# Linear attention and expert layer on one core: the keys of blocks 1 to 15 transposed by VectorE and 16 transfers instead of by TensorE, and the first block's orders rewritten

## The reference, cut to what matters

```python
def chunked_linear_attn(q, k, v):           # per chunk of 64 rows, per head
    inter  = einsum('bhcd,bhde->bhce', qq, state)
    scores = einsum('bhcd,bhed->bhce', qq, kk) * mask
    intra  = einsum('bhce,bhed->bhcd', scores, vv)
    state  = state + einsum('bhcd,bhce->bhde', kk, vv)
...
x = x + layernorm(attn(layernorm(x)))       # attn: q, k, v, the chunks, a norm per head, Wo
x = x + layernorm(ffn(layernorm(x)))        # ffn: sum over 8 experts of weight * Wd(silu(Wg x) * Wu x)
```

## Time and profile before

| | |
|---|---|
| median of 3 runs | 1467.39 us (1464.14 to 1468.72) |
| the profiled execution | 1467.63 us |
| its span | 1465.9 us |
| mean granted TensorE clock | 0.995 |
| TensorE busy | 1443.0 us (98%) |
| VectorE busy | 1027.0 us (70%) |
| ScalarE busy | 613.9 us (42%) |
| GpSimd busy | 428.4 us (29%) |
| DMA, share of its 16 engines by the packets of the main queue | 9.1% |

### The profile page before, as it was taken

The page is one execution under the profiler, slowest core; times in us unless marked ns, Lnnn a source line. Parts: engine busy times, 40 slices in busy tenths (PEclk is TensorE's granted clock), DMA queues, the critical chain, the costliest instruction groups (busy, mean ns, idle before and its releaser), DMA issues. The chain is left out here.

```text
span 1465.9 us, 37265 instructions
## 1 busy us (share of the span) xinstructions
PE 1443.0 (98%) x14076; PEld 1254.8 (86%) x14076; DVE 1027.0 (70%) x2459; ACT 613.9 (42%) x1159; POOL 428.4 (29%) x607
## 2 busy tenths in 40 slices
PE   7899999999999999999999999999999999999997
PEld 6788888888888888888888888888888888888887
DVE  6657768586686767768676686867768676685765
ACT  5443534444343343534344344443434445344432
POOL 1322414134241232414134241232413134241230
PEclk9999999999999999999999999999999999999999
DMA  5210100101001010100101001010100101000000
GB/s 173 73 16 6 32 7 14 29 14 29 0 14 29 14 29 0 34 9 14 29 14 29 0 14 29 14 29 0 31 12 14 29 14 29 0 15 16 1 8 22
DMA packets 106945, 32.53 MB, mean 22 GB/s; under 512 B 83616, under 2 KB 106656, under 8 KB 106912
## 3 DMA queue, kind: packets, MB, share of 16 engines
q1 hardware_dynamic: 106912, 32.08, 9.1%
HBM read 23.60 MB, written 8.39 MB: 22 GB/s over the span
## 5 line engine op out<-in xcount | busy, mean ns | idle before, releaser
L878 ACT ACTIVATE late<-gate_ps 128x512 f32<-128x512 f32 x256 | 153.2, 599 | 282.4 <-PE gate_ps L495 282.3
L495 PE MATMUL down_ps<-w_hi,h_hi 128*128 128x256 f32 x976 | 264.9, 294 | 0.0
L775 ACT ACTIVATE h_hi<-late 128x512 fp32r<-128x512 f32 x256 | 161.6, 631 | 235.5 <-DVE late L1125 235.5
L495 PE MATMUL down_ps<-w_hi,h_lo 128*128 128x256 f32 x976 | 254.4, 283 | 0.0
L1125 DVE TENSOR_TENSOR late<-late,up_ps 128x512 f32<-128x512 f32 x256 | 174.9, 683 | 112.1 <-PE up_ps L495 109.6
L1372 POOL TENSOR_TENSOR rms_in<-rms_in,minus_half 128x16 f32<-128x16 f32 x32 | 93.7, 2928 | 491.5 <-DVE rms_in L1073 491.5
L987 DVE TENSOR_TENSOR h_lo<-late,h_hi 128x512 fp32r<-128x512 f32 x256 | 175.6, 686 | 59.7 <-ACT h_hi L775 59.7
L1147 DVE SCALAR_TENSOR_TENSOR late<-down_ps,route,late 128x256 f32<-128x256 f32 x364 | 158.4, 477 | 82.2 <-PE down_ps L495 79.7
L495 PE MATMUL gate_ps<-ft_hi,w_hi 128*128 128x512 f32 x512 | 202.8, 396 | 1.6 <-ACT late L878 1.5
L495 PE MATMUL gate_ps<-ft_hi,w_lo 128*128 128x512 f32 x512 | 202.8, 396 | 0.0
L495 PE MATMUL up_ps<-ft_hi,w_lo 128*128 128x512 f32 x512 | 199.4, 389 | 0.0
(11 more groups left out here) (185 smaller groups left out, 2381.9 us busy)
## 6 DMA issues: line engine op xcount, KB each, us to landing
xs<-in_x SPq DMA_DIRECT2D x32, 256.0 KB, 2.9
out_rows<-late SPq DMA_DIRECT2D x32, 256.0 KB, 2.2
kz<-in_x SPq DMA_DIRECT2D x240, 32.0 KB, 1.8
late<-in_wg SPq DMA_DIRECT2D x7, 256.0 KB, 3.4
late<-in_wu SPq DMA_DIRECT2D x7, 256.0 KB, 4.5
late<-in_wd SPq DMA_DIRECT2D x6, 256.0 KB, 3.4
var_o<-var_s SPq DMA_DIRECT2D x60, 1.0 KB, 1.8
late<-in_wkv_t SPq DMA_DIRECT2D x1, 512.0 KB, 4.2
```

The costliest lines, as they stand in the source:

```text
L495: last = nc.tensor.matmul(dst, lhs, rhs, start=n == 0, stop=n == len(terms + low_terms) - 1)
L775: return nc.scalar.activation(dst, src, ACT.Copy)
L878: nc.scalar.activation(h_f[:, m, :], gate_ps[:, :], ACT.Silu).then_inc(silu_ready[0], 1)
```

## The change

The step "kt" leaves the places of the loop. In its stead VectorE turns the 32x32 blocks of `k_sb` into `rows` (step "k_turn", 4 instructions, at place 5), and SyncE places the turned blocks with 16 transfers of 32 KB from `rows` into `k_t`, the first half of `kz`, whose layout is changed (`place_keys`). The scores wait for all 16 (`k_placed`) instead of for ScalarE's copies. "kv" 1 and "q" 0 change places, so that both halves of the keys are there earlier. On SyncE, `place_keys` stands at the head of a pass, ahead of `load_x_t`. The first block keeps TensorE's transposes; its tables of order are written anew, and the matmuls that take the mean of the attention weights become steps of the table.

```diff
 STEPS = [
-    [("kv", 0), ("q", 0)],
+    [("kv", 0), ("kv", 1)],
     [],
-    [("q", 1), ("kv", 1)],
-    [("keep_x1",)],
-    [("kt", 0), ("kt", 1)],
+    [("q", 0), ("q", 1)],
+    [("keep_x1",), ("k_turn",)],
+    [],
...
-FIRST_PE = [("xt", 0), ("xt", 1), ("kv", 0), ("kv", 1), ("q", 0), ("su", 0), ("kt", 0), ("su", 1), ("q", 1), ("kt", 1),
+FIRST_PE = [("mean", "wkv"), ("xt", 0), ("mean", "wq"), ("xt", 1), ("kv", 0), ("q", 0), ("kv", 1), ("su", 0), ("kt", 0),
...
-FIRST_ACT = [("high", "wkv"), ("high", "wq"), ("xt", 0), ("high", "wo"), ("unit", 0), ("unit", 1), ("unit", 2), ("xt", 1),
+FIRST_ACT = [("xt", 0), ("high", "wkv"), ("xt", 1), ("high", "wq"), ("high", "wo"), ("unit", 0), ("unit", 1), ("kv", 0),
...
-        kz = sb("kz", [P, 2, HG, 2, 2 * P])
-        x_blocks = kz[:, :, :, 1, :]
+        kz = sb("kz", [P, 2, 2, HG, 2 * P])
+        k_t = kz[:, 0, :, :, :].rearrange("p h g c -> p (h g c)").rearrange("p (n c) -> p n c", c=P)
+        k_blocks = rows[:, :, :].rearrange("p t n -> p (t n)").rearrange("p (n c) -> p n c", c=P)
+        x_blocks = kz[:, 1, :, :, :]
...
+            def place_keys(block):
+                reach(sp, k_turned, block, 0)
+                for n in range(P // 32):
+                    for j in range(HPG):
+                        sp.dma_start(k_t[D * j:D * j + D, :, 32 * n:32 * n + 32],
+                                     k_blocks[32 * n:32 * n + 32, :, D * j:D * j + D]).then_inc(k_placed[0], 16)
...
             with sp.Fori(1, BLOCKS - 1) as i:
+                place_keys((i, 0))
                 reach(sp, blocks_turned, (i, 0), 0)
                 load_x_t(i * ROWS + ROWS)
...
+            place_keys((BLOCKS - 1, 0))
             store_out((BLOCKS - 2, 0), (BLOCKS - 2) * ROWS)
...
-                elif kind == "kt":
-                    p = step[1]
-                    reach(pe, k_ready, a, p + 1)
-                    for b in range(B):
-                        for g in range(HG):
-                            last = nc.tensor.transpose(dst[:, g, b * P:b * P + P], k_sb[:, 2 * p + b, g * P:g * P + P],
-                                                       ident[:, :])
                 elif kind == "s":
                     p = step[1]
                     reach(pe, q_ready, a, p + 1 if is_first(a) else HG)
-                    reach(pe, kz_ready, a, p + 1)
-                    if not is_first(a):
+                    if is_first(a):
+                        reach(pe, kz_ready, a, p + 1)
+                    else:
+                        reach(pe, k_placed, a, 0)
...
+                elif kind == "k_turn":
+                    reach(dve, k_ready, a, 2)
+                    for t in range(TILES):
+                        last = nc.vector.transpose(rows[:, t, :], k_sb[:, t, :])
+                    last.then_inc(k_turned[0], 1)
```

More of the change, by code:

```diff
@@ L96 @@
[L96 to L102, removed]
@@ new lines @@
+FIRST_DVE = [("x_stats", 0), ("x_stats", 1), ("x_norm", 0), ("centre", "wkv"), ("x_norm", 1), ("xt", 0), ("low", "wkv"),
+             ("centre", "wq"), ("scale", "wo"), ("xt", 1), ("low", "wq"), ("low", "wo"), ("unit", 0), ("unit", 1),
+             ("unit", 2), ("unit", 3), ("unit", 4), ("unit", 5), ("unit", 6), ("su", 0), ("su", 1), ("unit", 7),
+             ("unit", 8), ("s", 0), ("unit", 9), ("unit", 10), ("s", 1), ("unit", 11), ("unit", 12), ("norm_stats", 0),
+             ("unit", 13), ("unit", 14), ("unit", 15), ("norm_stats", 1), ("unit", 16), ("norm_apply", 0), ("unit", 17),
+             ("unit", 18), ("ot", 0), ("norm_apply", 1), ("unit", 19), ("ot", 1), ("unit", 20), ("ln2_stats", 0),
+             ("ln2_stats", 1), ("ln2_add", 0), ("ln3_stats", 0), ("ln2_add", 1), ("ln3_stats", 1), ("ln3_norm", 0),
+             ("ln3_norm", 1), ("ft_out", 0), ("ft_out", 1), ("unit", 21)]
@@ L107 @@
+FIRST_POOL = [("x_stats", 0), ("x_stats", 1), ("norm_stats", 0), ("norm_stats", 1), ("ln2_stats", 0), ("carry", 0),
+              ("ln2_stats", 1), ("ln3_stats", 0), ("ln3_stats", 1)]
+FIRST_WARM = {("kv", 0): 4, ("ot", 0): 16, ("ot", 1): 8, ("ft", 0): 27, ("ft", 1): 3}
 ROUTER, ROUTER_T = ("r",), ("rt",)
@@ L111, in psum_steps @@
     return [s for after in steps for s in after
-            if s[0] in ("q", "kv", "kt", "s", "o", "su", "ot", "wo", "ft")] + [ROUTER, ROUTER_T]
-PSUM_STEPS, FIRST_PSUM_STEPS = psum_steps(STEPS), [s for s in FIRST_PE if s[0] != "xt"] + [ROUTER, ROUTER_T]
+            if s[0] in ("q", "kv", "s", "o", "su", "ot", "wo", "ft")] + [ROUTER, ROUTER_T]
+PSUM_STEPS, FIRST_PSUM_STEPS = psum_steps(STEPS), [s for s in FIRST_PE if s[0] not in ("mean", "xt", "kt")] + [ROUTER, ROUTER_T]
 N_PSUM = len(PSUM_STEPS)
@@ L233, in build_program @@
         blocks_turned = counter("blocks_turned", 1)
+        kt_done = sem("kt_done")
+        k_turned = counter("k_turned", 1)
+        k_placed = counter("k_placed", 16 * HPG * P // 32)
         xt_loaded = counter("xt_loaded", 16 * B * KT * P // 32)
@@ L543, in att_step @@
                     last.then_inc(xt_done, 1)
+                elif step[0] == "mean":
+                    n, raw, columns = (0, wkv_raw, 2 * HID) if step[1] == "wkv" else (1, wq_raw, HID)
+                    pe.wait_ge(att_w_loaded[1 - n], 16)
+                    for k in range(KT):
+                        last = nc.tensor.matmul(up_ps[n][:, 0:columns], rz, raw[:, k, :], start=k == 0, stop=k == KT - 1)
+                    last.then_inc(mean_done, 1)
+                elif step[0] == "kt" and is_first(a):
+                    p = step[1]
+                    reach(pe, k_ready, a, p + 1)
+                    for b in range(B):
+                        for g in range(HG):
+                            last = nc.tensor.transpose(halves(up_ps[p][:, :])[:, g, b * P:b * P + P],
+                                                       k_sb[:, 2 * p + b, g * P:g * P + P], ident[:, :])
+                    last.then_inc(kt_done, 1)
                 if step not in PSUM_STEPS:
@@ L550, in att_step @@
                     pass
+                elif is_first(a) and number < 2:
+                    pe.wait_ge(xt_ready[0], number + 1)
                 elif number >= 2:
@@ L594, in att_step @@
                         tok, out_c = 2 * p * P + c, (b * HG + g) * C
-                        last = nc.tensor.matmul(score_banks(p)[C * i:C * i + C, j, out_c:out_c + C], kz[head, p, g, 0, c:c + C],
+                        last = nc.tensor.matmul(score_banks(p)[C * i:C * i + C, j, out_c:out_c + C], k_t[head, 2 * (2 * p + b) + g, C * i:C * i + C],
                                                 q_t[head, g, tok:tok + C], start=True, stop=True)
@@ L604, in att_step @@
                                     last = nc.tensor.matmul(dst[C * i:C * i + C, r, (4 * b + n) * C:(4 * b + n) * C + C],
-                                                            kz[half, p, g, j, c:c + C], q_t[half, g, tok:tok + C],
+                                                            kz[half, j, p, g, c:c + C], q_t[half, g, tok:tok + C],
                                                             start=True, stop=True)
@@ L728, in _ @@
             pe.wait_ge(const_ready, 1)
[L729 to L734, removed]
+            warm(2)
             for step in FIRST_PE:
@@ L820, in att_step @@
                 elif kind == "kt":
-                    if not is_first(a):
-                        copy(kz[:, step[1], :, 0, :], src).then_inc(kz_ready[0], 1)
-                        return
+                    act.wait_ge(kt_done, step[1] + 1)
                     for j in range(2):
-                        last = nc.scalar.activation(kz[:, step[1], :, j, :], src, ACT.Copy, scale=odd_even[:, j:j + 1])
+                        last = nc.scalar.activation(kz[:, j, step[1], :, :], halves(up_ps[step[1]][:, :]), ACT.Copy,
+                                                    scale=odd_even[:, j:j + 1])
                     last.then_inc(kz_ready[0], 1)
```

17 lines of the change are left out of this document (7 added, 10 removed).

## The result

The change takes 1505.89 us (median of 4 runs, 1504.94 to 1506.58) against 1467.36 us for the kernel before (median of 4, 1464.14 to 1468.72): 1.0265 times as long, with an interval from 1.0248 to 1.0283, or 38.5 us more. The profiled execution took 1505.44 us, with a span of 1503.7 us and a mean granted clock of 0.985.

What follows compares the result with a forecast made beforehand. TensorE's list of work was taken to bound the kernel; 1467.6 - 13.2 (transposes) + 34.5 (waits for keys) + 16 (clock) - 3 (first block) = 1502 us, range 1474 to 1518.

Steps and rivals of the forecast that it cites:

- TensorE's list: In blocks 1 to 15, the 8 transposes leave TensorE: 0.88 us per block, 13.2 us less in all.
- The turn on VectorE: Four block transposes per block take 1.41 us and fit in VectorE's 1.34 us wait before the next `hidden`, costing nothing.
- The price of an issue: On SyncE, each of the 16 key transfers takes 0.66 us to issue, one behind the other.
- The wait: In front of TensorE's scores, keys land 2.3 us late in each of fifteen blocks: 34.5 us more.
- The clock: TensorE's clock halves for 3.2 us after two waits in three, losing 1.6 us each: 16 us more.
- The first block: New order in block 0 starts its first product near 14.1 us: 3 us less, between 0 and 6.
- The bounds: Reasonable sums for the whole kernel, with waits of 1.4 to 2.8 us per block: lowest 1472 us, highest 1520 us.
- No wait at all: Rival: key issues take 0.50 us, TensorE meets no wait, its clock stays, 1451 us; chance 0.10.
- A short wait: Rival: issues near 0.56 us, wait of 0.8 us before the scores, too short for the clock, 1463 us; chance 0.05.
- The rule of the Trainium skill on issue time: Rival: starting a DMA is usually short beside the DMA, so SyncE's issues overlap, no wait, 1451 us; chance 0.03.
- The queue was not late as well: Rival: `place_keys` slips behind `store_out` on SyncE past 184.15; two us beyond give about 1532 us; chance 0.03.

Runs made afterwards that it cites:

- the first experiment: The turn of the keys one place earlier on VectorE, at place 4, against the changed kernel: 1451.33 us, 0.9892 of the kernel before.

## Why the prediction was right

The forecast was 1502 us in 1474 to 1518; 1505.9 us was measured. The mechanism is the one that was forecast: late keys, 15 waits, and a clock that falls behind some of them. That the sum lies so close is in part luck, since errors cancel: against its own terms the waits were 5.4 us more, the two waits without a releaser 1.9 more, and the first block 3.8 less. Step by step:

- **TensorE's list** (-13.2): 88.23 - 87.37 = 0.86 us a pass, -12.9.
- **The turn on VectorE** (0): it took 1.42 us and filled the gap, and the first experiment moved it into another gap without cost.
- **The price of an issue** (0.66 us, from the four of `place_var`, against 0.50 from x): 10.61 us for 16, 0.66 each. The row with both ends in SBUF was the right one to price from; the run out of HBM takes 0.48, and half the pieces per transfer changed next to nothing, as was argued.
- **The wait** (2.3 us, 34.5 in all): 2.51 to 2.58 us in 13 of the 15, 39.9 in all. Of the 5.4 us that were missing, 3.2 are those 13 (0.25 us each, most of it the landing), and 2.2 the first and the last: there the 16 issues took 11.58 and 11.16 us, and the waits 3.61 and 3.16.
- **The clock** (two waits in three, 1.6 us each, 16): 10 of 15, about 1.5 us each, more in the first: 14.7 + 1.5 = 16.2 by the passes, 14.6 by the traces with the idle time filled. The low stretch is as long as was assumed (3.3 us, 3.2 in the earlier trace rows). That two in three came out to the unit is luck: nothing in the prediction told which waits the clock would follow, and in the trace it fell behind some and not behind others of the same length. That the clock falls after such a wait, and what it costs, was in the earlier trace rows.
- **The first block** (-3, 0 to 6): -3.05 by the runs, -6.8 in the one trace, which is outside the bounds given, and -4.9 with the two waits without a releaser, which give a part of it back. The first product came at 12.86, where the prediction had near 14, and the stretch at half the clock behind it (16.80 to 20.00 in the earlier trace rows) is gone, as was held possible. What was not counted is the second such stretch, which before lasts from 37.3 to 44.0 us and in the change from 36.0 to 39.4.
- **The bounds.** The highest sum leaves out the -3 and the lowest has it: with the first block's own bounds, 0 and 6, the lowest is 1469. This does not touch the forecast.
- **The rivals.** No wait at all needed issues of 0.5 us: in these runs they exist only with a source in HBM. A short wait leaves the clock alone, as this rival held (the run with 14 transfers), but it needed issues that are shorter than they are. The rule of the Trainium skill on issue time (the section named above) did not hold for 16 small transfers in a row: 10.61 us of issues against one landing of 2.0. The queue was not late as well: `store_out` ended at 177.97, 5.1 us ahead of the keys.

## What to carry to other kernels

A step that is cut into many small transfers should be costed as a chain: the end of what feeds it, plus the number of issues times the pitch of the nearest row of the same kind, plus one landing, held against the time at which the reader would come. If it is late by a few us, first look for an earlier place for the step that feeds it, or let a second engine issue a part; both took the wait away here, but for 0.5 to 0.7 us in the first pass or the last block. And where the reader is the engine that bounds the kernel, its idle time costs more than itself as soon as the clock falls behind it.

## What was not expected of the hardware

- SyncE's time for an issue hung on where the source lies (0.66 us from SBUF, 0.48 from HBM) and hardly on the size: half the pieces took 10.47 instead of 10.61 us for 16.
- A small difference in idle time changed the clock's answer from none to all: with waits of 1.2 us (the first and the last 2.1 and 2.3) it fell in 0 of 15 windows, with 2.3 us (3.0 and 3.0) in 9, with 2.5 us (3.6 and 3.2) in 10, with 4.5 us (6.1 and 5.7) in 15. Between these ends the length of the wait alone does not decide: behind two waits of 2.54 us it stayed once and fell once.
- Where code runs for the first time the traces show extra time: an issue of the keys of up to 1.29 us instead of 0.61 (the first pass and the last block take 11.58 and 11.16 us for 16), and waits of TensorE of 0.5 to 2.5 us put down to "issue" in the first block, the first pass and the last block. That it is the first run of the code that costs this is not shown: what TensorE waits for there no row shows, and it was not tried.
